# A cross-attention block: interleaved stack rows, and inverse sums turned once and spread by four transfers

## The reference

```python
tgt1 = _layer_norm(tgt, g1, be1)
# _self_attn: q, k, v from tgt1, 16 heads
score = jnp.einsum('bshd,bthd->bhst', q, k) / math.sqrt(HD)
score = score + (1.0 - mask[:, None, :, :]) * -1000000000.0
p = jax.nn.softmax(score, axis=-1)
o = jnp.einsum('bhst,bthd->bshd', p, v).reshape(b, s, d)
tgt = tgt + (o @ Wo.T + bo)
tgt = tgt + (memory @ Wg.T + bg)
tgt1 = _layer_norm(tgt, g2, be2)
ff = jax.nn.relu(tgt1 @ W1.T + b1) @ W2.T + b2
return tgt + ff
```

## Time and profile before

| | |
|---|---|
| Time, median of 3 runs | 1809.25 us (1807.23 to 1810.44) |
| The profiled execution | 1808.42 us, span 1806.8 us |
| PE busy | 1752.8 us, 97% |
| ACT, DVE, POOL busy | 81%, 75%, 49% |
| Mean granted TensorE clock | 0.990 |
| DMA, mean busy share of queue 1 | 60.6% |
| HBM | 62.73 MB read, 16.78 MB written |

### The profile page before, as it was taken

How to read it: one execution, slowest core, us unless ns; L and a number is a source line. 1 busy time by engine, 2 the same in 40 slices (tenths; PEclk the granted TensorE clock), 3 DMA queues, 4 the chain that set the end, 5 groups by cost and what they waited for, 6 DMA issues and landing times.

```text
span 1806.8 us, 53745 instructions
## 1 busy us (share of the span) xinstructions
PE 1752.8 (97%) x17972; PEld 1717.7 (95%) x17972; DVE 1356.8 (75%) x6807; ACT 1455.3 (81%) x5577; POOL 876.4 (49%) x910
## 2 busy tenths in 40 slices
PE   5699999999999999999999999999999999999997
PEld 5699999999999999999999999999999999999997
DVE  6677777777777777777777777777777777777772
ACT  4788888787787887888787887887888888887882
POOL 4254454454454455455454454444544444454454
PEclk7899999999999999999999999999999999999999
DMA  7665765755765755755755755755755756756740
GB/s 165 94 94 99 119 93 99 118 92 98 121 91 95 124 89 98 123 89 99 124 88 99 123 88 100 123 87 101 124 85 101 121 87 103 117 90 104 112 72 19
DMA packets 148931, 183.66 MB, mean 102 GB/s; under 512 B 14768, under 2 KB 99120, under 8 KB 148656
## 3 DMA queue, kind: packets, MB, share of 16 engines
q1 hardware_dynamic: 148656, 180.23, 60.6%
HBM read 62.73 MB, written 16.78 MB: 44 GB/s over the span
## 4 chain that ended last, share of the span: by engine, by line
PE 94%; ACT 1%; issue 1%; DMA 0%; DVE 0%; SPq 0%; ACTq 0%
PE ffn_ps L807 13%; PE ffn_ps L808 13%; PE ffn_ps L809 13%; PE turn_ps L873 12%; PE work_ps L807 9%; PE work_ps L809 8%; PE work_ps L808 8%; PE score_ps L859 7%; PE value_ps L899 6%; PE work_ps L824 3%; PE turn_ps L883 2%; ACT scores L374 1%; DMA k_stack<-k_hi 0%; ACT hid L419 0%; SPq L325 0%
## 5 line engine op out<-in xcount | busy, mean ns | idle before, releaser
L374 ACT ACTIVATE scores<-scores,row_min 128x128 f32<-128x128 f32 x2048 | 795.4, 402 | 0.8 <-DVE row_min L608 0.8
L733 POOL TENSOR_TENSOR hT_lo<-hid,hT_hi 128x512 fp32r<-128x512 f32 x256 | 355.5, 1389 | 552.5 <-DVE hT_hi L635 552.5
L386 ACT ACTIVATE probs<-turn_ps 128x512 f32<-128x512 f32 x512 | 305.2, 597 | 254.7 <-PE turn_ps L873 254.7
L608 DVE CUSTOM_DVE_ANT_0 scores<-score_ps,mask_bias 128x128 f32<-128x128 f32 x2048 | 471.5, 286 | 1.9 <-issue 1.9
L374 ACT ACTIVATION_READ_ACCUMULATOR scores<-scores,row_min 128x1 f32 x2048 | 412.7, 202 | 0.0
L873 PE MATMUL turn_ps<-ident,scores 128*128 128x128 f32 x2048 | 308.3, 273 | 5.9 <-ACT probs L386 5.9
L807 PE MATMUL ffn_ps<-zT_hi,w_lo 128*128 128x256 f32 x1024 | 302.3, 295 | 5.0 <-ACT hid L419 4.1
L807 PE MATMUL ffn_ps<-w_hi,hT_lo 128*128 128x256 f32 x1024 | 300.7, 294 | 2.4 <-ACT hid L419 2.4
L808 PE MATMUL ffn_ps<-zT_lo,w_hi 128*128 128x256 f32 x1024 | 285.5, 279 | 0.0
L809 PE MATMUL ffn_ps<-zT_hi,w_hi 128*128 128x256 f32 x1024 | 284.9, 278 | 0.0
L809 PE MATMUL ffn_ps<-w_hi,hT_hi 128*128 128x256 f32 x1024 | 284.6, 278 | 0.0
(11 more groups left out here) (113 smaller groups left out, 4242.2 us busy)
## 6 DMA issues: line engine op xcount, KB each, us to landing
q_stack<-q_hi SPq DMA_DIRECT2D x128, 256.0 KB, 6.8
k_stack<-k_hi SPq DMA_DIRECT2D x256, 128.0 KB, 7.3
x_in<-x_dram SPq DMA_DIRECT2D x64, 256.0 KB, 3.7
mem_in<-memory_dram SPq DMA_DIRECT2D x64, 256.0 KB, 7.9
x_res<-x_dram SPq DMA_DIRECT2D x64, 256.0 KB, 7.9
q_stack<-q_lo SPq DMA_DIRECT2D x64, 256.0 KB, 4.2
k_stack<-k_lo SPq DMA_DIRECT2D x128, 128.0 KB, 7.3
out_dram<-y SPq DMA_DIRECT2D x64, 256.0 KB, 2.2
```

What stands on the lines that cost most here:

```text
L374: last = act.activation(exps, exps, ACT.Exp, bias=row_min[:, k, h:h + 1], scale=-1.0, accum_out=row_sum[:, k, h:h + 1])
L386: act.activation(probs[:, k, :], turn_ps[k % 2][:, :], ACT.Copy).then_inc(probs_copied, 1)
L608: last = dve.tensor_tensor_reduce(out=scores[:, slot(i, t), h, :], in0=score_ps[t % 2][:, h * S:(h + 1) * S], in1=mask_bias[:, b, :], scal ...
L733: pool.tensor_tensor(halves[1], src, halves[0], ALU.subtract).then_inc(done, 1)
```

## The change

Two things are changed. First, the stacks' rows are interleaved: term j of q now lies at partitions j, j+4, j+8, ..., and term j of half e of k at partitions 64e+j, 64e+j+4, and so on. Sizes, sources and the order of the nine transfers stay. The zero rows are then every fourth, so the first clearing covers all of q_stack.

Second, the inverse sums. DVE writes each inverse four times (`COPIES` = 4; two instructions of 32 values per batch element in place of one of 16), so that all 16 heads of both batch elements fill exactly 128 columns. PE turns this one block, and does it at the end of tick 12 of the same iteration rather than in tick 0 of the next. ACT copies 128 columns to `inv_cols` at tick 12. SP then issues four transfers (`SPREADS`) at the end of its iteration: each reads 32 partitions of `inv_cols`, each row four times, and writes 128 partitions by 128 columns of `inv`, 64 KB. DVE's multiplication at tick 2 now waits for these transfers. POOL's repetition (L724) is gone. The setup tile `be1w` moves to `resid_b2`, since `inv_rows` is gone.

```diff
@@ -83,6 +83,8 @@
     HALF = CPB * HD
+    COPIES = P // (GB * H)
+    SPREADS = GB * KT
     assert S == P and D == 2 * P and CHUNKS == 8 and HJ == 4
@@ -139,8 +141,8 @@
         scores = sb("scores", [P, RING, CH, S])
-        inv_rows = sb("inv_rows", [P, GB, KT, P])
-        be1w = inv_rows[:, 0]
+        sum_inv = sb("sum_inv", [P, GB, KT, CPB, 2, COPIES])
+        inv_cols = sb("inv_cols", [P, S])
         probs = sb("probs", [P, CHUNKS, CH * S])
@@ -150,6 +152,7 @@
         resid_b2 = sb("resid_b2", [P, GB, D])
+        be1w = resid_b2[:, :, 0:P]
         hid = sb("hid", [P, 2, 2, ROWS])
@@ -167,7 +170,6 @@
         bqc, bkc = qk_bias[:, 0:KT], qk_bias[:, KT:2 * KT]
-        sum_inv = sb("sum_inv", [P, GB, KT, CPB, 2])
         mv1, mv2 = sb("mv1", [P, GB, 2]), sb("mv2", [P, GB, 2])
@@ -316,13 +318,13 @@
                     for j, high_low in enumerate((1, 0, 0)):
-                        sp.dma_start(q_stack[g % 2][32 * j:32 * j + 32].bitcast(F32),
+                        sp.dma_start(q_stack[g % 2][j:P:CPB].bitcast(F32),
                                      q[high_low][:].bitcast(F32)).then_inc(q_stacked, 16)
...
                         for j, high_low in enumerate((0, 1, 0)):
-                            to = 32 * j + HD * e
-                            sp.dma_start(k_stack[g % 2][to:to + HD, :, e].bitcast(F32),
+                            to = HALF * e + j
+                            sp.dma_start(k_stack[g % 2][to:HALF * (e + 1):CPB, :, e].bitcast(F32),
                                          kk[high_low][HALF * e:HALF * (e + 1)].bitcast(F32)
@@ -345,6 +347,18 @@
                     sp.dma_start(out_rows[i - 2], y[:]).then_inc(y_stored, 16)
+                if attn_:
+
+                    sp.wait_ge(inv_copied, i + 1)
+                    if later(i):
+                        sp.wait_ge(attn_ready, i)
+                    heads = P // SPREADS
+                    for b in range(GB):
+                        for k in range(KT):
+                            at = heads * (KT * b + k)
+                            sp.dma_start(inv[:, k, b * S:(b + 1) * S],
+                                         inv_cols[at:at + heads, :].unsqueeze(1)
+                                         .broadcast_to([heads, P // heads, S])).then_inc(inv_spread, 16)
@@ -390,16 +404,13 @@
                 if later(g):
-                    act.wait_ge(attn_ready, g)
-                act.activation(inv[:].rearrange("p k r -> p (k r)"), turn_ps[0][:, :], ACT.Copy
-                               ).then_inc(inv_copied, 1)
+                    act.wait_ge(inv_spread, 16 * SPREADS * g)
+                act.activation(inv_cols[:], turn_ps[0][:, 0:S], ACT.Copy).then_inc(inv_copied, 1)
...
                         copy_turned(i - 1, CHUNKS - 1)
-                    if out_ and t == 1:
-                        copy_inverses(i - 1)
                     if front and t == 0:
@@ -447,6 +458,8 @@
                         exponentials(i, EXP_TICKS.index(t))
+                    if attn_ and t == 12:
+                        copy_inverses(i)
@@ -547,9 +560,12 @@
                 if later(i):
-                    dve.wait_ge(inv_spread, GB * (i - 1) + b + 1)
-                dve.reciprocal(sum_inv[:, b], row_sum[:, CPB * b:CPB * (b + 1), :]
-                               .rearrange("p c (k e) -> p k c e", k=KT)).then_inc(sums_inverted, 1)
+                    dve.wait_ge(inv_turned, i)
+                for k in range(KT):
+                    last = dve.reciprocal(sum_inv[:, b, k],
+                                          row_sum[:, CPB * b:CPB * (b + 1), 2 * k:2 * k + 2]
+                                          .unsqueeze(3).broadcast_to([P, CPB, 2, COPIES]))
+                last.then_inc(sums_inverted, 1)
@@ -619,7 +635,7 @@
                         dve.wait_ge(attended, g + 1)
-                        dve.wait_ge(inv_copied, g + 1)
+                        dve.wait_ge(inv_spread, 16 * SPREADS * (g + 1))
                         if later(g):
@@ -688,7 +704,7 @@
             def set_zeros(n):
-                pool.memset(q_stack[n][96:P].rearrange("p r k n -> p (r k n)").bitcast(F32), 0.0
+                pool.memset(q_stack[n][:].rearrange("p r k n -> p (r k n)").bitcast(F32), 0.0
                             ).then_inc(zeros_set, 1)
@@ -716,17 +732,6 @@
-            def spread_inverses(g, b):
-
-                pool.wait_ge(sums_inverted, GB * g + b + 1)
-                if later(g):
-                    pool.wait_ge(inv_turned, g)
-                pool.tensor_tensor(inv_rows[:, b].rearrange("p k (h d) -> p (k h) d", d=HD),
-                                   sum_inv[:, b].rearrange("p k c e -> p (k c e)").unsqueeze(2)
-                                   .broadcast_to([P, H, HD]),
-                                   one[:, :].unsqueeze(2).broadcast_to([P, H, HD]), ALU.mult
-                                   ).then_inc(inv_spread, 1)
-
             def split_low(src, halves, high, count, done):
@@ -740,10 +745,6 @@
                                   HJ * g + n + 1, hid_split)
-                    if attn_ and t == 6:
-                        spread_inverses(i, 0)
-                    if attn_ and t == 10:
-                        spread_inverses(i, 1)
                     if out_ and t == 2:
@@ -876,13 +877,10 @@
-                pe.wait_ge(inv_spread, GB * (g + 1))
+                pe.wait_ge(sums_inverted, GB * (g + 1))
                 pe.wait_ge(probs_copied, CHUNKS * g + CHUNKS - 1)
-                for k in range(KT):
-                    for b in range(GB):
-                        last = pe.transpose(turn_ps[0][:, k * ROWS + b * S:k * ROWS + (b + 1) * S],
-                                            inv_rows[:, b, k, :], ident[:])
-                last.then_inc(inv_turned, 1)
+                pe.transpose(turn_ps[0][:, 0:S], sum_inv[:].rearrange("p b k c e n -> p (b k c e n)"),
+                             ident[:]).then_inc(inv_turned, 1)
@@ -914,7 +912,6 @@
                         turn_chunk(i - 1, CHUNKS - 1)
-                        turn_inverses(i - 1)
                     if front and t == 0:
@@ -984,6 +981,8 @@
                             last.then_inc(down_ready, 1)
+                    if attn_ and t == 12:
+                        turn_inverses(i)
```

## The result

The changed kernel takes 1763.39 us (median of four runs; one of them took 4054.56 us, and the ratio leaves it out), against 1809.32 us before: a ratio of 0.9747, with a 95% interval of 0.9728 to 0.9766. The direction was forecast, the size was not: 1776 us was predicted, with 1766 as the lower end. The profiled execution's span went from 1806.8 to 1761.2 us, by 45.6 us.

The account below looks back on a forecast made before the run. It took two nearly equal loops to bound the kernel: PE's work, and scores through q stack to next scores. 21.1 + 9.3 + 3 = 33.4 us off 1808.42 gave 1775, plus 0.8 for the median: 1776; range 1766 to 1791.

Parts of the forecast that it names:

- the two loops: PE's own work, and scores through q product and stack transfers to the next scores: nearly equal, the second 27.25 us.
- PE's transposes, 21.1 us: Between first scores and q product, three of four transposes go: 0.33 us in each of 64 groups.
- The interleaved rows help enough: Stack transfers get faster by at least 3% of some 13 us, 0.4 us per iteration, enough to end PE's wait.
- The stack's wait, 9.3 us: PE's wait ahead of the scores, 33 seams in the waits table, vanishes: 9.3 us gained in all.
- The start, 3 us: At the kernel's start, where PE waits longer for stacks, faster stacks give 3 us; bounds 0 to 10.
- DVE, +0.92 us: Four reciprocals of 32 values replace two of 16: 0.92 us more DVE work per iteration, at no cost in time.
- ACT's copy: The copy of inverses shrinks from 512 to 128 columns and takes 0.4 us, off the path.
- The inverse transfers cost nothing: DVE waits 0 to 0.65 us for the four transfers; a delay up to 1.35 us is swallowed.
- The case of stacks at twice the rate: Rival: stack transfers take about half the time, the start gives some 7 us: 1772 us, chance 15%.
- Its sign of 26.7 us between two q issues: If the forecast holds, successive q stack issues lie about 26.7 us apart, against 27.25 before.
- the stretch at 919 us: In the trace before the change, k stack transfers were read as moving at 131 GB/s there.

Follow-up runs that it names:

- e1: The kernel before with the interleaved stack rows alone, the inverses as before: 1782.06 us, ratio 0.9856.
- e2: The changed kernel with the stack rows put back on neighbouring partitions, so the inverses' change alone: 1778.67 us, ratio 0.9838.
- e4: The changed kernel with PE turning the block of inverses four times instead of once: 1783.78 us, ratio 0.9864.
- e5: The changed kernel with three more 32 KB transfers per iteration ahead of the four inverse transfers: 1767.33 us, ratio 0.9774.
- e6: The changed kernel with six more 32 KB transfers per iteration ahead of the four inverse transfers: 1869.47 us, ratio 1.0337.

## Why the prediction was wrong

Its steps, one by one.

- **What bounds the kernel, and the two loops.** Right. e1 and e2 show both: each takes away part of one and the same lateness. Wrong was that both loops lose 0.33 us: the second lost 0.44, as the transpose that stays is not in it (e2).
- **PE's transposes, 21.1 us.** Right: 19.7 us by the chain in 60 iterations, 20.4 by e4.
- **The interleaved rows help enough.** Right, and by far more than the 3% wanted; landing 2.3 us.
- **The stack's wait, 9.3 us.** This is the step that failed, the term of the sum read from the waits table: "PE has no other wait there". The late stack cost 18.4 us in the middle part (19.0 by e1). The table counts only time in which PE stands still, and it took the matmul ahead for busy until its end. It was to be seen in the trace of before. One seam that was not late, and an ordinary one in which the chain has no wait either:

```profile
193.53 0.47 PE score_ps L859 x4
...
954.43 0.68 PE score_ps L859 x4
```

  The timelines of PE and of its weight loads show where the 0.21 us are (start, us, what; first the seam that was not late, then the other):

```profile
193.25 0.28 PE L809 MATMUL ffn_ps<-w_hi,hT_hi 128*128 128x256 f32 x1
193.37 0.63 PE L859 MATMUL score_ps<-k_stack,q_stack 128*128 128x256 f32 x4
...
193.25 0.54 PEld L859 LDWEIGHTS score_ps<-k_stack,q_stack 128*128 128x128 f32 x4
...
954.15 0.28 PE L809 MATMUL ffn_ps<-w_hi,hT_hi 128*128 128x256 f32 x1
954.40 0.71 PE L859 MATMUL score_ps<-k_stack,q_stack 128*128 128x256 f32 x4
...
954.37 0.54 PEld L859 LDWEIGHTS score_ps<-k_stack,q_stack 128*128 128x128 f32 x4
```

  On time, the first score matmul starts 0.12 us after the start of the matmul ahead (193.37 less 193.25). At 954 its weights come 0.2 us late and it starts after 0.25 us. Yet no idle time is counted, since the matmul ahead has a duration of 0.28 us in the profile. So the table misses the first 0.16 us of every late start (0.28 less 0.12). Beyond that only the second score matmul follows later than usual, after 0.19 us for 0.12; the third and fourth keep their pace. Over the 61 seams behind 95 us the scores took 0.659 us on the chain before and take 0.475 now: 0.184 us per seam, or 11.2 us that the waits table leaves to the scores. With 10.4 us of waits on the chain (43 seams; the table has 9.3 in 33) this makes 21.6 us, of which the 60 iterations hold 21.1; PE's slower products take 2.7 us of it back. In PEld's row the hint was open: 17.8 us of idle time in 44 cases, against PE's 9.3 in 33.
- **The start, 3 us.** 6.8 us (e1: 7.3 us). Nearly all of it lies at the two stops of the earlier trace rows: the scores that started at 57.39 and 82.38 us start at 54.74 and 76.22. The bounds were 0 to 10; I chose low because of other late work. e2, without faster stacks, gains 0.8 us there.
- **DVE, +0.92 us.** 4 x 0.322 - 0.502 = 0.79 us; a value costs 4.4 ns between 16 and 32 values (251 and 322 ns), where I took 6.5. Hidden, as said: the k transfers follow the q transfers by 3.54 us for 3.49, not by 0.45 us more. **ACT's copy** 0.28 us for 0.4.
- **The inverse transfers cost nothing.** Right in the result: they land after 2.1 us, DVE waits 0.45 us on average and at most 1.6 (100 to 1700 us), nothing on PE. The Trainium skill (DMA: Bandwidth & Descriptors, "Anatomy of one DMA"), which the prediction cites, gives the 2.0 us for transfers issued from GpSimd; these come from SP, and their 2.1 us agree with it. Wrong in the slack: 1.35 us was that of the q stack, which fast stacks no longer need; it is over 2.4 us, by estimate some 2.9 (e5, e6).
- **The rivals.** The case of stacks at twice the rate gave 1772 us; they came at three times, and it had the same 9.3 us in it. With 18.4 for 9.3 and 6.8 for 3 the forecast's own sum would have been 1808.4 - 21.1 - 18.4 - 6.8 = 1762.1 us, against 1762.95 for the profiled execution; this closes the account and proves nothing, as both new terms are read from the result. Its sign of 26.7 us between two q issues came out at 26.53. And the stretch at 919 us, read there as k's rate, still has the last of q in it; from 920 to 926 k moves at 107 to 131 GB/s.

So the mechanism was right, and two terms came out at about half of what was measured: the stack's wait (9.3 for 18.4 us) and the start (3 for 6.8).

## What to carry to other kernels

When PE waits for an operand, price the wait from the start of the matmul ahead to the end of the group behind, not by the idle time, and compare with the same group where it was not late. Two changes that lessen one wait don't add up, and each one's own gain isn't its share. With transfers between partitions of on-chip memory, look at which partitions a transfer writes, before sizes and counts; and count SP's issue time, 0.6 to 0.7 us for each of these transfers, as a resource of its own.

## What the runs showed of the hardware that I had not expected

- A transfer of 256 KB with 128 rows of 2 KB to 32 partitions moves at 133 GB/s to 32 neighbours or to every second of 64, and at 402 GB/s to every fourth of 128. One of 128 KB to 16 partitions: 107 to 131 GB/s to neighbours, 218 to 230 to every second of 32.
- Late weights make four matmuls of 256 columns take 0.71 us of the chain, 0.24 us more than the 0.47 of an undisturbed seam, beside the wait: 0.16 us of it is lateness hidden by the duration that the profile gives the matmul ahead, the rest the later second matmul.
- A transpose on DVE in 32 x 32 blocks, 128 x 64 values, takes 246 ns; a reciprocal of 32 values per partition 322 ns (16: 251).
